# Choosing the slot inside the dynamics product, the centre tap as a sign, and parameters loaded in another order

## The reference

```python
x = x + conv_ref(gn(x), w1, b1, fscale, conv_bias)

def gn(v, G=32, eps=1e-05):            # 32 groups of one channel each
    return (v - mean(v)) / sqrt(var(v) + eps)

def conv_ref(x, w1, b1, fscale, conv_bias):
    avg = x.mean(axis=(2, 3))                               # (16, 32)
    dyn = avg @ w1.T + b1                                   # (16, 288)
    wk = sigmoid(dyn).reshape(b * c, 1, 3, 3)
    y = conv(x, wk, padding=1, one channel per group) + conv_bias
    return (x - y) * fscale * x + y
```

## Time and profile before

| | |
|---|---|
| median of 3 runs | 272.12 us (271.8 to 272.37) |
| the profiled execution's own time | 272.44 us |
| its span | 270.7 us |
| PE busy | 237.2 us (88%), PEld 183.5 (68%) |
| DVE busy | 236.0 us (87%) |
| ACT busy | 213.4 us (79%) |
| POOL busy | 227.5 us (84%) |
| mean granted clock of PE | 0.992 |
| memory traffic | 39.31 MB read, 37.75 MB written |
| the chain that ended last | POOL 65%, issue 14%, PE 12%, DMA 4%, DVE 2% |

### The profile page before, as it was taken

How to read it: one execution, slowest core, us unless ns; L and a number is a source line. 1 busy time by engine, 2 the same in 40 slices (tenths; PEclk the granted TensorE clock), 3 DMA queues, 4 the chain that set the end, 5 groups by cost and what they waited for, 6 DMA issues and landing times.

```text
span 270.7 us, 9000 instructions
## 1 busy us (share of the span) xinstructions
PE 237.2 (88%) x3506; PEld 183.5 (68%) x3506; DVE 236.0 (87%) x569; ACT 213.4 (79%) x386; POOL 227.5 (84%) x258
## 2 busy tenths in 40 slices
PE   0018997997999999999999999999999999999991
PEld 0014784785868686868677777868686877778670
DVE  2737789799999999999999999999999999755645
ACT  2116877698898989989898989898998989899520
POOL 0044266969999999999999999999999999999982
PEclk9999999799999999999999999999999999999999
DMA  7999901298498979799897979797979744444466
GB/s 262 336 404 426 402 30 68 110 338 372 170 353 324 353 296 367 282 357 351 292 399 261 385 278 381 298 362 290 372 277 374 319 177 178 176 178 174 179 274 251
DMA packets 10371, 77.64 MB, mean 287 GB/s; under 512 B 1265, under 2 KB 1496, under 8 KB 2648
## 3 DMA queue, kind: packets, MB, share of 16 engines
q1 hardware_dynamic: 10328, 77.06, 74.4%
HBM read 39.31 MB, written 37.75 MB: 285 GB/s over the span
## 4 chain that ended last, share of the span: by engine, by line
POOL 65%; issue 14%; PE 12%; DMA 4%; DVE 2%; SPq 1%; ACT 0%; POOLq 0%; DVEq 0%; ACTq 0%
POOL outs L841 46%; POOL inv_std L798 9%; PE conv_ps L426 7%; DMA gates<-gate 4%; PE conv_ps L432 2%; POOL tap L832 2%; POOL roots L824 1%; POOL avg L812 1%; POOL moments L808 1%; POOL square L806 1%; PE conv_ps L488 1%; POOL moments L803 1%; POOL numbers L822 1%; DVE outs L576 1%; SPq L314 1%
## 5 line engine op out<-in xcount | busy, mean ns | idle before, releaser
L426 PE MATMUL conv_ps<-xs,taps 64*64 64x448 f32 x1536 | 226.2, 555 | 2.5 <-DVE taps L550 1.5
L841 POOL TENSOR_TENSOR outs<-outs,linear 128x1152 f32<-128x1152 f32 x63 | 166.1, 2645 | 1.6 <-DVE outs L576 1.4
L432 PE MATMUL conv_ps<-xs,taps 64*64 64x128 f32 x1536 | 122.0, 273 | 0.0
L426 PEld LDWEIGHTS conv_ps<-xs,taps 64*64 64x64 f32 x1536 | 107.6, 134 | 20.3 <-issue 7.0
L576 DVE SCALAR_TENSOR_TENSOR outs<-xs,beta,conv_ps 128x576 f32<-128x576 f32 x128 | 102.6, 802 | 16.9 <-PE conv_ps L426 16.6
L713 ACT ACTIVATE linear<-xs,slope 128x576 f32<-128x576 f32 x128 | 109.4, 858 | 3.2 <-POOL outs L841 3.2
L432 PEld LDWEIGHTS conv_ps<-xs,taps 64*64 64x64 f32 x1536 | 102.1, 134 | 12.3 <-issue 6.1
L523 DVE BATCH_NORM_STATS2 pieces<-xs 128x6 f32<-128x64 f32 (+1 forms) x256 | 102.6, 451 | 5.1 <-DMA xs<-x 5.1
L688 ACT ACTIVATE xs<-xs,shift 128x594 f32<-128x594 f32 x128 | 99.4, 780 | 0.0
L798 POOL TENSOR_TENSOR inv_std<-numbers,minus_half 128x8 f32<-128x8 f32 x16 | 26.4, 1648 | 4.5 <-ACT dev_mean L694 4.5
L543 DVE TENSOR_TENSOR taps<-dyn_ps,tap 128x1512 f32<-128x1512 f32 (+1 forms) x19 | 27.9, 1481 | 2.1 <-POOL tap L832 2.1
(11 more groups left out here) (59 smaller groups left out, 153.7 us busy)
## 6 DMA issues: line engine op xcount, KB each, us to landing
xs<-x SPq DMA_DIRECT2D x30, 1188.0 KB, 11.0
out<-outs SPq DMA_DIRECT2D x30, 1152.0 KB, 5.2
xs<-x SPq DMA_DIRECT2D x4, 594.0 KB, 5.6
out<-outs SPq DMA_DIRECT2D x3, 576.0 KB, 2.9
out<-outs SPq DMA_DIRECT2D x2, 288.0 KB, 2.6
cst<-const SPq DMA_DIRECT2D x1, 248.0 KB, 7.0
w1s<-w1r SPq DMA_DIRECT2D x1, 115.9 KB
gates<-gate SPq DMA_DIRECT2D x1, 8.0 KB
```

Of the source, the lines that this page charges most:

```text
L426: return nc.tensor.matmul(tile(i, g, taken)[:, START:BANK], taps[given, i % 2, at:at + HALF], xs[given, i % XBUFS, g, 0:PAIRED, 1 + shift: ...
L432: return nc.tensor.matmul(tile(i, g, half)[:, BANK:END], taps[half, i % 2, at:at + HALF], xs[half, i % XBUFS, g, PAIRED:BLOCKS, 1 + shift: ...
L841: nc.gpsimd.tensor_tensor(tile, tile, linear[:, PAIR * k:PAIR * (k + 1)].rearrange("p g n -> p (g n)"), ALU.add).then_inc(out_ready, 1)
```

## The change

**The slot.** The rows of averages are kept four times, in a tile of 4 x 129 columns that POOL clears once. ACT's copy writes, for slot s, only the columns of the partitions of that slot, every fourth one; the others stay zero. The weights are laid out slot by slot, 72 columns each, and the dynamics product is a sum over the four slots into 72 columns of PSUM: a partition gets only its own slot's terms. The rows of -1e30 and the sum over slots go, and so does `own_taps` on DVE; the sigmoid writes 72 columns, and POOL's `scaled_taps` reads them.

**The sign.** Sigmoid minus one is the negative of the sigmoid of the negated argument. At the start ACT turns the sign of the centre taps' weights, in place (`turn_weights`, three operations), and the band holds -1 instead of 1 there. Since only the middle shift k holds the centre, the band becomes three bands of 64 columns, one for each shift.

**The loads.** The gates come ahead of the constants, with a semaphore of their own; the weights come last and fill 128 rows instead of 103.

```diff
-BIASES = TAPS * C + TAPS
-INPUTS = BIASES + SLOTS
-NEVER = -1e30
+INPUTS = TAPS * C + TAPS
...
-for _name, _width in (("average", PARTS), ("band", HALF), ("centre", GROUPS * SETS),
+for _name, _width in (("average", PARTS), ("band", TAPS * HALF), ("turn", TAPS),
                       ("spread", INPUTS), ("phase", PARTS), ("counts", 1)):
     _AT[_name] = (_N, _N + _width)
...
-    band = ((slot[:, None] == m % SLOTS) & (np.abs(row[:, None] - m // SLOTS) <= 1)).astype(np.float32)
+    near = ((slot[:, None] == m % SLOTS) & (np.abs(row[:, None] - m // SLOTS) <= 1)).astype(np.float32)
+    band = np.stack([near, near, near], axis=1)
+    band[:, 1] -= 2 * ((slot[:, None] == m % SLOTS) & (row[:, None] == m // SLOTS))
     put("band", band)
 
-    centre = np.zeros((PARTS, GROUPS, TAPS, TAPS), np.float32)
-    for p in range(PARTS):
-        centre[p, :, 1, phase[p]] = -1.0
-    put("centre", centre)
...
+
+    giver_of = np.full(PARTS, TAPS)
+    giver_of[:TAPS * C] = np.arange(TAPS * C) // C
+    giver_of[TAPS * C:INPUTS] = np.arange(TAPS)
+    put("turn", 1.0 - 2.0 * (giver_of[:, None] == np.arange(TAPS)))
...
-    wr = np.zeros((TAPS, SLOTS, GROUPS, GROUPS, TAPS, TAPS, SLOTS), np.float32)
-    br = np.zeros((TAPS, GROUPS, TAPS, TAPS, SLOTS), np.float32)
+    wr = np.zeros((TAPS, SLOTS, GROUPS, SLOTS, GROUPS, TAPS, TAPS), np.float32)
+    br = np.zeros((TAPS, SLOTS, GROUPS, TAPS, TAPS), np.float32)
...
-                wr[ph, :, :, :, k, q, :] = w[:, :, kh, TAPS - 1 - k].transpose(2, 3, 1, 0)
-                br[ph, :, k, q, :] = b[:, :, kh, TAPS - 1 - k].transpose(1, 0)
-    other = np.broadcast_to(NEVER * (1 - np.eye(SLOTS, dtype=np.float32))[:, None, :], (SLOTS, GROUPS * SETS, SLOTS))
-    wr = np.concatenate([wr.reshape(TAPS * C, -1), br.reshape(TAPS, -1), other.reshape(SLOTS, -1)]).astype(np.float32)
+                wr[ph, :, :, :, :, k, q] = w[:, :, kh, TAPS - 1 - k].transpose(2, 3, 0, 1)
+                br[ph, :, :, k, q] = b[:, :, kh, TAPS - 1 - k]
+    rest = np.zeros((PARTS - INPUTS, SLOTS * GROUPS * SETS), np.float32)
+    wr = np.concatenate([wr.reshape(TAPS * C, -1), br.reshape(TAPS, -1), rest])
...
-        w1s = sb("w1s", [INPUTS, GROUPS * SETS * SLOTS])
+        w1s = sb("w1s", [PARTS, SLOTS, GROUPS * SETS])
...
-        avg_rows = sb("avg_rows", [INPUTS, PARTS])
-        sig = sb("sig", [PARTS, GROUPS * SETS, SLOTS + 1])
-        less_one = sb("less_one", [PARTS, GROUPS * SETS])
+        avg_rows = sb("avg_rows", [PARTS, SLOTS * (PARTS + 1)])
+        sig = sb("sig", [PARTS, GROUPS * SETS])
...
-        band_ps = dyn_ps[:, 320:320 + HALF]
+        band_ps = dyn_ps[:, 128:128 + TAPS * HALF]
...
             load_first()
+            sp.dma_start(gates[:].rearrange("p a g -> p (a g)"), gate).then_inc(gates_loaded, 16)
             sp.dma_start(cst[:], const).then_inc(consts_loaded, 16)
-            sp.dma_start(w1s[:], w1r).then_inc(params_loaded, 16)
-            sp.dma_start(gates[:].rearrange("p a g -> p (a g)"), gate).then_inc(params_loaded, 16)
+            sp.dma_start(w1s[:].rearrange("p s t -> p (s t)"), w1r).then_inc(weights_loaded, 16)
             for i in range(1, XBUFS):
                 load(i)
...
+            def rows_of(rows, s, cols):
+                return avg_rows[rows, s * PARTS + cols.start:s * PARTS + cols.stop]
+
...
             def dynamics_whole(j):
                 pe.wait_ge(constants_set, 1)
+                pe.wait_ge(weights_turned, TAPS)
                 pe.wait_ge(avg_rows_ready, j + 1)
-                nc.tensor.matmul(dyn_ps[:, 0:GROUPS * SETS * SLOTS], avg_rows[:], w1s[:],
-                                 start=True, stop=True).then_inc(dyn_done, 1)
+                for s in range(SLOTS):
+                    ins = nc.tensor.matmul(sums_ps, rows_of(slice(0, INPUTS), s, slice(0, PARTS)), w1s[0:INPUTS, s],
+                                           start=s == 0, stop=s == SLOTS - 1)
+                ins.then_inc(dyn_done, 1)
...
             def dynamics_first(j):
                 at_least(pe, matrices_ready, matrix_steps(j))
                 pe.wait_ge(avg_rows_ready, j + 1)
-                for cols in (TOP, BOTTOM):
-                    nc.tensor.matmul(dyn_ps[cols, 0:GROUPS * SETS * SLOTS], avg_rows[TOP, cols], w1s[TOP],
-                                     start=True, stop=False).then_inc(dyn_half, 1)
+                for s in range(SLOTS):
+                    for cols in (TOP, BOTTOM):
+                        nc.tensor.matmul(sums_ps[cols], rows_of(TOP, s, cols), w1s[TOP, s],
+                                         start=s == 0, stop=False).then_inc(dyn_half, 1)
 
             def dynamics_second(j):
-                pe.wait_ge(dyn_half, 2 * j)
-                for cols in (TOP, BOTTOM):
-                    nc.tensor.matmul(dyn_ps[cols, 0:GROUPS * SETS * SLOTS], avg_rows[HALF:INPUTS, cols], w1s[HALF:INPUTS],
-                                     start=False, stop=True).then_inc(dyn_done, 1)
+                rest = slice(HALF, INPUTS)
+                pe.wait_ge(dyn_half, 2 * SLOTS * j)
+                for s in range(SLOTS):
+                    for cols in (TOP, BOTTOM):
+                        nc.tensor.matmul(sums_ps[cols], rows_of(rest, s, cols), w1s[rest, s],
+                                         start=False, stop=s == SLOTS - 1).then_inc(dyn_done, 1)
...
-            pe.wait_ge(params_loaded, 32)
             dynamics_whole(0)
...
-            def own_taps(j):
-                dve.wait_ge(sig_ready, j + 1)
-                nc.vector.tensor_reduce(less_one[:], sig[:], AX_X, ALU.add).then_inc(less_one_ready, 1)
-
...
-                    band_ps[:, 0:TRIPLES * TAPS].rearrange("p (a q) -> p a q", q=TAPS).unsqueeze(1).unsqueeze(1).to_broadcast(shape),
+                    bands[:, :, 0:TRIPLES * TAPS].rearrange("p k (a q) -> p k a q", q=TAPS).unsqueeze(1).to_broadcast(shape),
...
-                    band_ps[:, HALF - 1:HALF].unsqueeze(1).to_broadcast([PARTS, GROUPS, TAPS]),
+                    bands[:, :, HALF - 1].unsqueeze(1).to_broadcast([PARTS, GROUPS, TAPS]),
...
-            nc.vector.tensor_copy(sig[:, :, SLOTS], const_of("centre")).then_inc(centres_filled, 1)
             for g in range(GROUPS):
                 bn(1, g)
-            dve.wait_ge(centres_filled, 1)
-            own_taps(0)
             rows(1)
             first_matrices()
...
                     product(0, 4)
-                    own_taps(1)
                     bn(3, 1)
...
-                    if nxt and i > 1:
-                        own_taps(i + 1)
                     bn_ahead(i + 3, 1, 2)
...
-                    if i == 1:
-                        own_taps(2)
                     bn_ahead(i + 3, 3, 4)
...
             def copy_averages(j):
                 act.wait_ge(avg_rows_done, 2 * j + 1)
-                nc.scalar.activation(avg_rows[:], avg_ps, ACT.Identity).then_inc(avg_rows_ready, 1)
+                if j == 0:
+                    act.wait_ge(rows_cleared, 1)
+                nc.scalar.activation(avg_rows[0:INPUTS].rearrange("p (s w) -> p s w", w=PARTS + 1)[:, :, 0:PARTS:SLOTS],
+                                     avg_ps.rearrange("p (m s) -> p s m", s=SLOTS),
+                                     ACT.Identity).then_inc(avg_rows_ready, 1)
 
             def sigmoid(j):
-                act.wait_ge(dyn_done, 2 * j + 1)
-                at_least(act, less_one_ready, j)
-                nc.scalar.activation(sig[:, :, 0:SLOTS], dyn_ps[:, 0:GROUPS * SETS * SLOTS].rearrange("p (a c) -> p a c", c=SLOTS),
-                                     ACT.Sigmoid).then_inc(sig_ready, 1)
+                act.wait_ge(dyn_done, 2 * SLOTS * j + 1)
+                at_least(act, tap_ready, j)
+                nc.scalar.activation(sig[:], sums_ps, ACT.Sigmoid).then_inc(sig_ready, 1)
+
+            def turn_weights():
+                act.wait_ge(consts_loaded, 16)
+                act.wait_ge(weights_loaded, 16)
+                turned = w1s[:].rearrange("p s (g k q) -> p (s g) k q", k=TAPS, q=TAPS)
+                for q in range(TAPS):
+                    nc.scalar.activation(turned[:, :, 1, q], turned[:, :, 1, q], ACT.Identity,
+                                         scale=const_of("turn")[:, q:q + 1]).then_inc(weights_turned, 1)
...
+            turn_weights()
             count(0)
             negative_mean(0)
...
             nc.gpsimd.memset(shift[:, :, 0], -1.0).then_inc(ones_set, 1)
-
-            pool.wait_ge(params_loaded, 32)
+            nc.gpsimd.memset(avg_rows[:], 0.0).then_inc(rows_cleared, 1)
+
+            pool.wait_ge(gates_loaded, 16)
             nc.gpsimd.tensor_scalar(neg_fs[:], gates[:, 0], -1.0, None, ALU.mult).then_inc(sides_ready, 1)
...
             def scaled_taps(j):
-                pool.wait_ge(less_one_ready, j + 1)
+                pool.wait_ge(sig_ready, j + 1)
                 at_least(pool, matrices_ready, matrix_steps(j))
-                nc.gpsimd.tensor_tensor(tap[:], less_one[:].rearrange("p (g t) -> p g t", g=GROUPS),
```

(16 more changed lines are left out.)

## The result

The changed kernel takes 266.12 us in the median of four runs (265.5 to 266.61), against 272.03 before: 0.9776 of it, 95% interval 0.976 to 0.9792. The profiled execution took 265.87 us, its span is 263.9. The kernel before has no single time: of its 48 runs beside the experiments, 41 with a mean granted clock of 0.988 to 0.992 took 271.6 to 272.7 us, and 7 with 0.996 took 270.3 to 270.7.

The account below looks back on a forecast made before the run. POOL was taken to pace the middle, after a start chain waiting for the gates; 4.2 us from the start plus 1.5 from the reduction, others 0, made 5.7 us off 272.12: 266.4 us, range 263.3 to 270.5.

Parts of the forecast that it names:

- The gates and weights: At the start: gates landed by 10, weights at 11.3, turning them 1.0 us, `count(0)` at 12.3.
- from there to the sigmoid the chain is as long as before: Image 0 at the start: from moments at 14.4 to sigmoid at 21.4, as 18.29 to 25.30 before.
- best: At the start: earliest expected landing of x of image 1, 14; worst 18.3, and 15.6 was taken.
- Term 1: At the start: earlier gates and weights bring the first convolution to 24.5 from 28.71, -4.2 us (bounds -2.3, -5.2).
- term 2: In the ramp: POOL's `tap(1)` waits for the sigmoid itself, not DVE's reduction; a further -1.5 us (0 to -1.8).
- term 3: In the ramp: POOL's waits before 58.12 and 60.08 stay about as long; 0 us (-2.0 to +1.0).
- Both of these rivals: In the ramp: PE takes half the gain back, about 269.5, chance 0.13; all POOL's waits go, 264.4, chance 0.12.
- POOL without idle time from about 55 on: Sign expected in the trace: after the ramp POOL never stands idle, at 14.57 us an image.
- The middle: In the steady images: PE's dynamics product costs 0.5 us more an image (0 to 3.2), with no effect on the time.
- that cover hides it: In the middle: PE's loader wait of 1.08 us an image for POOL's moments absorbs PE's extra 0.5 us.
- The rival of PE as the bound: In the middle: PE's extra work beyond 1.08 us is paid 13 times; 278 to 294 us, chance 0.07.
- POOL paces the middle: In the middle: POOL's 52 large adds run without idle time before them, setting 14.57 us an image.

Follow-up runs that it names:

- The run with the copy: The changed kernel with a plain DVE copy of the sigmoid where the reduction stood, POOL's taps waiting for it; 275.33 us, 1.0134 of the kernel before.

## Why the prediction was right, step by step

The forecast was 266.4 us and 266.12 came; the place of the gain was right as well, most of it from the start. Several steps were off and cancelled.

- *The gates and weights:* 9.89 for "by 10", turning from 10.92 for 11.3; `count(0)` at 11.65 for 12.3, since the weights were there earlier and the turning held it up for 0.73 us and not 1.0. The step "from there to the sigmoid the chain is as long as before" failed: 13.88 to 21.63 is 7.75, not 7.01. The first product, eight passes instead of two, takes 1.96 us in place of 1.30 (from PE's timeline before):

```profile
23.96 1.30 PE L399 MATMUL dyn_ps<-w1s,avg_rows 103*128 103x288 f32 x2 [0.46 <-ACT avg_rows L698]
```

  The two errors left the moments 0.5 early and `tap(0)` 0.2 late. x of image 1 landed at 13.7, better than the "best" of 14. The first convolution came at 25.04 for 24.5: warm-up products stood until 25.11, which the forecast didn't see, as they stood there before too. Term 1, -4.2, is -3.7 there and -4.4 at the first add.
- *The reduction, term 2:* -1.5 at `tap(1)` came as -1.6. But what it is worth at the end was mis-sized: the run with DVE's step back in its place lost 0.3 (medians) to 0.9 (ratios), within the noise.
- *POOL's later waits, term 3:* forecast 0; 1.5 of the 2.0 went, and 0.72 was given back between `tap(3)` and `tap(4)` (15.31 us, for 14.59 before), where POOL waits for PE's means. Both of these rivals were half true, and the sign "POOL without idle time from about 55 on" failed at 67.30. The granted clock, for which the forecast counted nothing, stayed up.
- *The middle:* 0.5 us an image more for PE was close (0.43). The cover was not: "that cover hides it", 1.08 us. The room was 0.45, and the change took nearly all of it; the loader's wait didn't shrink to 0.6 as forecast but went. The time came out as forecast only because 0.43 is just under 0.45. The rival of PE as the bound was far nearer than its 0.07 said.
- *What bounds it:* "POOL paces the middle" was true by 0.28 us; that POOL's adds never wait showed that it paces, not by how much.
- *The sum:* 5.7 us were forecast; the traces show 6.75 at `tap(15)` and 6.57 between the two profiled executions, and only the medians differ by 5.9. That the forecast came within 0.3 us is in part luck.

Not settled: how the 1.8 us of the slots divide between DVE's shorter order, the wait for it, PE's longer product and the clock; and whether 99 rows are faster than 128 (in the profiled execution with 99, x of image 0 landed 0.4 us earlier, 4.81 for 5.22).

## What to carry to other kernels

A wait in the profile isn't room: an engine made slower there may wait elsewhere, so give it extra work, or its rival less, and see from where the period grows. A small load ahead of large ones is worth a look at its number of rows, and a gain in a ramp counts only as far as the next engine keeps it.

## What the runs showed of the hardware

The run with the copy shows what it waits for. A plain copy of 72 columns on DVE took 0.19 to 0.20 us in the four places where no large add ran on POOL when it began, and 1.20 to 2.25 us in the twelve where one ran; each of these twelve ended within 0.1 us of the end of that add (here 97.76 + 1.42 = 99.18, and 96.48 + 2.64 = 99.12). From the timelines of DVE and POOL:

```profile
21.64 0.20 DVE L546 COPY less_one<-sig 128x72 f32<-128x72 f32 x1 [2.34 <-ACT sig L718]
...
97.76 1.42 DVE L546 COPY less_one<-sig 128x72 f32<-128x72 f32 x1
```

```profile
96.48 2.64 POOL L865 TENSOR_TENSOR outs<-outs,linear 128x1152 f32<-128x1152 f32 x1
```

A reduction with as many elements took 0.22 to 0.24 in all 16 places. The Trainium skill (SBUF — State Buffer, "Terms") says that VectorE and GpSimd share a pair of ports that one of them holds for a whole instruction, while the other is blocked; the copy's ends agree with that. The reduction did not wait.

A pass of 72 columns added among PE's others cost 0.031 us (16 of them: 0.50) and 0.041 (32: 1.32).
